# Masked attention on one core: the fourth and fifth token tile transposed in the first two steps of the fifth head, the third pair's values behind them

## The reference, cut to what matters

```python
xt = jnp.transpose(x, (0, 2, 1))
q = xt @ Wq.T
qh = q.reshape(B, T, NH, dk).transpose(0, 2, 1, 3)
scores = scale * jnp.einsum('bhqd,bhkd->bhqk', qh, qh)
logits = (scores * cmask + (1.0 - cmask) * NEG) * rmask
attn = jax.nn.softmax(logits, axis=-1)
ctx = jnp.einsum('bhqk,bhkd->bhqd', attn, qh)
out = ctx @ Wo.T
return x + transpose(out)
```

## Time and profile before

| | |
|---|---|
| median of three runs | 1621.71 us (1619.72 to 1621.74) |
| the profiled execution, and its span | 1617.55 us, 1615.8 us |
| TensorE / its weight loads | 95% / 76% of the span |
| GpSimd / VectorE / ScalarE | 83% / 73% / 53% |
| granted TensorE clock, mean | 0.981 |

### The profile page before, as it was taken

The page is one execution under the profiler, slowest core; times in us unless marked ns, Lnnn a source line. Parts: engine busy times, 40 slices in busy tenths (PEclk is TensorE's granted clock), DMA queues, the critical chain, the costliest instruction groups (busy, mean ns, idle before and its releaser), DMA issues. The chain is left out here.

```text
span 1615.8 us, 33177 instructions
## 1 busy us (share of the span) xinstructions
PE 1537.4 (95%) x10956; PEld 1222.4 (76%) x10956; DVE 1185.3 (73%) x2659; ACT 854.3 (53%) x2055; POOL 1339.1 (83%) x1069
## 2 busy tenths in 40 slices
PE   6798999999999999999999999999999999999995
PEld 3666777787877788787777777777877777777863
DVE  5356787877778787787878778787877778787773
ACT  2145556565555556555555655555555565555450
POOL 5558989898898989889898988989898898987771
PEclk9689999999999999999999999999999999999997
DMA  3434455454544545353554535445554544453410
GB/s 115 107 85 96 105 129 122 110 130 99 129 103 123 122 110 136 93 135 97 123 122 114 136 93 132 100 120 122 123 128 98 129 106 119 115 131 90 109 50 30
DMA packets 93810, 179.09 MB, mean 111 GB/s; under 512 B 24704, under 2 KB 24832, under 8 KB 93632
## 3 DMA queue, kind: packets, MB, share of 16 engines
q1 hardware_dynamic: 64448, 109.71, 30.0%
q0 software_dynamic: 29184, 67.17, 14.9%
HBM read 36.77 MB, written 33.55 MB: 44 GB/s over the span
## 5 line engine op out<-in xcount | busy, mean ns | idle before, releaser
L870 DVE TENSOR_REDUCE small_mxp<-max_scores 108x1 f32<-108x270 f32 x1280 | 546.7, 435 | 269.9 <-PE max_scores L1069 245.4
L751 ACT ACTIVATE small_Pt<-scores,small_kbias 108x270 f32<-108x270 f32 x1280 | 551.5, 483 | 343.9 <-PE scores L1088 335.9
L596 POOL TENSOR_TENSOR small_Pacc<-small_Pacc,small_Pt 108x540 f32<-108x540 f32 x384 | 517.8, 1349 | 117.1 <-ACT small_Pt L751 110.3
L1069 PE MATMUL max_scores<-small_ops 128*108 128x270 f32 x1280 | 412.0, 329 | 17.3 <-DVE small_mxp L870 16.3
L1100 PE MATMUL ctx_psum<-small_Pt,small_V 108*64 108x270 f32 x2560 | 313.1, 391 | 0.0
L900 DVE RECIPROCAL small_rsum<-small_rsum 128x67 f32<-128x67 f32 (+1 forms) x512 | 240.8, 532 | 77.6 <-ACT small_rsum L698 75.8
L1069 PEld LDWEIGHTS max_scores<-small_ops 128*108 128x108 f32 x1280 | 218.9, 173 | 86.3 <-issue 41.0
L1085 PE MATMUL scores<-small_ops 128*108 128x270 f32 x1280 | 270.8, 290 | 4.7 <-ACT small_Pt L751 4.5
L1100 PEld LDWEIGHTS ctx_psum<-small_Pt,small_V 108*64 108x64 f32 x2560 | 184.3, 137 | 106.9 <-issue 0.2
L1088 PE MATMUL scores<-small_ops 128*108 128x270 f32 x1280 | 263.6, 287 | 0.0
L1085 PEld LDWEIGHTS scores<-small_ops 128*108 128x108 f32 x1280 | 191.5, 173 | 25.5 <-ACT small_Pt L751 8.8
(11 more groups left out here) (108 smaller groups left out, 2366.2 us busy)
## 6 DMA issues: line engine op xcount, KB each, us to landing
small_ops<-small_H SPq DMA_DIRECT2D x512, 135.0 KB, 2.8
small_ops<-small_L SPq DMA_DIRECT2D x256, 135.0 KB, 2.7
small_ops<-small_mrow SPq DMA_DIRECT2D x128, 2.1 KB
small_xg<-x_rows,small_idx POOLq DMA_INDIRECT x80, 3.9
small_xtail<-x_rows,small_idx POOLq DMA_INDIRECT x80, 4.9
out_rows<-small_xtail,small_idx POOLq DMA_INDIRECT x80, 3.8
out_rows<-small_xg,small_idx POOLq DMA_INDIRECT x80, 3.8
wq_sb<-wq SPq DMA_DIRECT2D x1, 1024.0 KB, 5.3
```

What stands on the lines that cost most here:

```text
L596: nc.gpsimd.tensor_tensor(acc, other, t["Pt"][:R, p0], ALU.add).then_inc(pacc_step, 1)
L751: nc.scalar.activation(t["Pt"][:R, (NT * s + k) % f.NP, half, :], ST[(2 * (NT * h + k) + half) % 3][:R, 0:H], ACT.Exp, bias=t["kbias"][:R, ...
L870: nc.vector.tensor_reduce(t["mxp"][:R, h % 2, m // 2, m % 2:m % 2 + 1], MX[m % 2][:R, 0:H], AX.X, ALU.max).then_inc(mx_red, 1)
L1069: nc.tensor.matmul(MX[m % 2][:R, 0:H], ops[:, OPA, tile_cols(m // 2)], ops[:, OPB, half_cols(m % 2)], start=True, stop=True).then_inc(mx_r ...
```

## The change

Two entries of one table and one of another are altered. In the fifth head, the fourth tile's transposes go from step 1 to step 0 (part 0), the fifth tile's from step 2 behind the group to step 1 (part 0). The third pair's values go from step 0 (first job in part 0, second in part 1) to step 1 part 1 and step 2 part 1, there behind the group. Every engine takes its share of a job from the same tables, so the copies and residuals move along, and the banks are dealt out anew.

```diff
--- before.py
+++ after.py
@@ -43,8 +43,8 @@
     ((3, 3), (3, 4), "out", 4),
     ((4, 3), (4, 3), "proj", (4, 0)), ((4, 4), (4, 4), "proj", (4, 1)), ((5, 3), (5, 4), "proj", (5, 0)),
     ((6, 0), (6, 1), "proj", (5, 1)), ((7, 0), (7, 1), "proj", (6, 0)), ((7, 3), (7, 4), "w", 0)]
-V_STEPS = {1: ((0, 2, 1), (0, 3, 0)), 2: ((4, 0, 0), (4, 0, 1)), 3: ((5, 0, 0), (5, 1, 0)), 4: ((6, 3, 0), (6, 4, 0))}
-XT_STEPS = [(1, 2, 1), (2, 2, 1), (3, 2, 1), (4, 1, 0), (4, 2, 1)]
+V_STEPS = {1: ((0, 2, 1), (0, 3, 0)), 2: ((4, 1, 1), (4, 2, 1)), 3: ((5, 0, 0), (5, 1, 0)), 4: ((6, 3, 0), (6, 4, 0))}
+XT_STEPS = [(1, 2, 1), (2, 2, 1), (3, 2, 1), (4, 0, 0), (4, 1, 0)]
 XBAR_STEP = (6, 2, 1)
 MT_AT = 1
 CTX_HIGH_AT = {(0, 4): 3, (4, 1): 0, (4, 4): 1, (6, 4): 2}
```

## The result

The changed kernel took 1627.99 us (median of six, 1623.98 to 1628.85) against 1621.34 us before (1619.54 to 1621.74), a ratio of 1.0037 with an interval of [1.0025, 1.0050]: slower, by more than the 0.2% of no change. Run again beside the kernel before, it gave 1625.38 against 1620.76, ratio 1.0027 [1.0018, 1.0037]. The time of 1622.1 that I forecast was too low, and "within 0.2%" was the wrong case; the range reached to 1628.0, and that the measured median lies 0.01 us inside it is luck. Of the ten executions of experiment 4's kernel one took 2151.57 us at a mean clock of 0.652, and the ratio given there is of the other nine.

The account below looks back on a forecast made before the run. TensorE's queue was taken to bound each batch. 14 x 0.04 - 1.06 + 0.72 = +0.2 us on the median 1621.71 gave 1621.9, and half the collision (0.2 us) made it 1622.1; range 1616.0 to 1628.0.

Parts of the forecast that it names:

- within 0.2%: Whole kernel: time differs from the kernel before by no more than 0.2%, 3.2 us; chance 0.59.
- What goes: Pair 4's projection (L1133) no longer waits for VectorE's residual (L892) of the last tile: -0.88 us a batch.
- What comes: Fifth head's first two steps: values job waits for the fourth tile's residual, +0.93 us; middle batch nets +0.04 us.
- The sign for it: New wait of values (L1179) for the residual (L892), 14 times, 0.7 to 0.9 us listed idle.
- What the moved work passes: Fifth head: row sums and group stay hidden by 0.3 and 0.5 us; GpSimd's step 3 sum comes later.
- Off TensorE's path, at nothing: GpSimd's step 3 sum, at about 710.05 instead of 709.22, is absorbed by its later jobs and costs nothing.
- Collision: VectorE's context residual (L905) overlaps GpSimd's later token sum, ending up to 1.0 us later: 0 to +0.3 us a batch.
- The sign for C: L905's mean above 900 ns, for the rival where TensorE pays the collision, 0.1 to 0.6 us a batch; chance 0.22.
- The rule on the ports: VectorE and GpSimd share SBUF ports under an exclusive lock; by it the hold of L905 is certain where they overlap.
- First batch: The 0.73 us wait goes and two matmuls replace four transposes, GpSimd's wait covering the new chain: -1.06 us.
- Last batch: No transposes or projection; the eight values matmuls leave a place where TensorE then waits for VectorE's reduction: +0.72 us.

Follow-up runs that it names:

- experiment 4: Changed kernel with VectorE's second finishing operation (L948) of the fifth output tile cut to 2 of 512 columns; 1620.67 us, ratio 0.9984 to the kernel before.
- experiment 9: Changed kernel with third pair's values back ahead of the transposes, and VectorE's first context residual (L905) moved from (4, 4) to (4, 3); 1610.16 us, ratio 0.9935.
- x10_after_low: Changed kernel with VectorE's first context residual (L905) moved from (4, 4) to (4, 3); 1621.83 us, ratio 0.9999 to the kernel before.
- x5_keep_v_swap: Changed kernel with values back ahead of transposes, GpSimd's token sums of (4, 3), (4, 4) exchanged with scatters of (5, 0), (5, 1); 1721.44 us, ratio 1.0622.
- experiment 12: The changed kernel run again unaltered, for the spread, beside the kernel before; 1625.38 us (1622.77 to 1628.84).
- x6_swap: Changed kernel with GpSimd's token sums of (4, 3), (4, 4) exchanged with its scatters of (5, 0), (5, 1); 1728.21 us, ratio 1.0662.
- x11_before_low: Kernel before with VectorE's first context residual (L905) moved from (4, 4) to (4, 3); 1621.92 us, ratio 1.0008.
- x7_before_swap: Kernel before with GpSimd's token sums of (4, 3), (4, 4) exchanged with its scatters of (5, 0), (5, 1); 1640.30 us, ratio 1.0126.

## Why the prediction was right in part and wrong in part, by its steps

- **What goes:** right. L1133 no longer waits for L892 in any batch, and the wait that was put at 0.88 us was worth that: experiment 9, which has no stall in its place, lasts 92.80 us a batch against 93.66 in most batches before.
- **What comes:** right. Values 3.37 us behind the head's start by the sum (703.45 - 700.08), 3.29 measured; the projection 8.84 to 8.90 by the sum, 8.83 measured. Experiment 4 shows that it hangs on VectorE's finishing operations. Trace and sum agree within 0.1 us because all durations came from rows of the same stretch. With the collision out of the way (x10_after_low) a batch is 0.08 us shorter than before, where the sum had +0.04 with bounds of -0.15 and +0.25. The sign for it, a listed wait of L1179 in every batch, failed, though what it stood for came.
- **What the moved work passes:** the row sums and the group stand for nothing new, as said. GpSimd's sum for step 3 comes 9.99 us behind the head's start instead of 9.14, the 0.85 us that were forecast. "Off TensorE's path, at nothing" is the step that failed: it was at nothing for the row sums, and not for L905.
- **Collision:** the term that was mis-sized, and paid at another place. The prediction bounded it at 0 to 0.3 us a batch and then put half of that, about 0.2 us, into the whole sum, where it belongs into each of 14 batches: its own half would have been 2.1 us and the forecast 1624.0. Measured are 0.37 us a batch for the holds (0.30 net), 4.2 us net in 14. Its mechanism was right for the first place (0.80 us measured, up to 1.0 forecast), but what it left to be paid there, about 0.3 us, was in fact nothing. The second place, which it didn't follow, is held 0.40 us and paid, because GpSimd's next token sum has moved too. That 0.3 a batch stands in both is luck. The sign for C, a mean of L905 above 900 ns, came true: 1084 ns, 808 before.
- **The rule on the ports:** the rule of the Trainium skill that the prediction weighed (SBUF — State Buffer, "SBUF: two separate sides", an exclusive lock on the pair of ports shared by VectorE and GpSimd, held for the whole instruction by the one that starts first) agrees with the holds of the changed kernel, where each ends 0.57 us behind the end of a token sum (719.20 + 1.51 against 720.14, 722.64 + 1.11 against 723.18). It doesn't give the 6.87 us of x5_keep_v_swap, where VectorE stays held over four more instructions of GpSimd that start behind it. Which of two starts first, rows 0.03 us apart don't settle. I should have let the rule set the likeliest case. That it is this lock and no other bond of the two engines, no run here shows.
- **First batch:** -1.06 us forecast; +2.33 in the first profiled execution of the changed kernel and +0.27 in the second. The stall that goes did go. What covers the gain is the clock's lower level, which the profile of before doesn't have there, and the forecast had no such term. In the second execution it came at a place where TensorE would have waited for GpSimd anyway. Why it comes, and whether the changed kernel has it more often, is open.
- **Last batch:** +0.72 us forecast, +0.76 from the wait at (6, 1) of the batch before to the first output matmul of the last (103.14 - 102.38). The wait that takes the place of the values is 0.67 us ahead of the odd maximum of (4, 1), at 1555.58. The row that the forecast reckoned from, at 1554.08, belongs to the sixth head and not to the fifth; that the size came out is luck.

Sum of what the traces show: 4.2 + 0.76 = 4.9 us, and 0.3 to 2.3 us of the first batch. The two comparisons have 6.65 and 4.62 us between their medians. In experiment 12 the executions at a mean clock of 0.979 or more have medians 2.9 us apart (1623.42 and 1620.48), those below it 4.9 (1626.48 and 1621.61). The profiled executions of the changed kernel are also 3.9 and 3.4 us late at the first listed wait for a maximum, before any moved job. That is start-up and not the change: x6_swap, with the same tables for the moved jobs, is only 0.4 us late there, and x11_before_low, without the change, 2.6.

## What to carry to other kernels

When work moves in a kernel whose engines are all near full, redo not only the waits but the overlaps: list the VectorE operations with two inputs in SBUF and what GpSimd does at the same moment, before and after. Moving a job so that it no longer waits for an engine is worth nothing if its bank is handed to it by the same engine; ask which order leaves each bank to the job whose releaser is done first. A hold costs nothing where idle time of the held engine follows (+0.80 us in (4, 4)), and is paid in full where none does (+0.87 us in (5, 1) of x7_before_swap).

## What was not expected of the hardware

- VectorE's operation with two SBUF inputs can be held across several GpSimd operations: 6.87 us behind five without a gap (x5_keep_v_swap), where in the changed kernel it got in after one (1.51 us). In 13 batches of x5_keep_v_swap its row starts from 0.03 us ahead of GpSimd's first to 0.02 behind it, and it is held over all five each time; in x7_before_swap it is held over five where it starts 0.08 us ahead, and gets in after one in the 13 batches where it starts 0.3 us into a sum. One batch of x6_swap breaks the pattern: 0.01 us ahead, and in after one (1.89 us). What decides is open.
- The issue of a scatter on GpSimd doesn't hold it: the first L905 of x5_keep_v_swap, at 750.16, takes 0.71 us beside the scatter at 750.01.
- GpSimd is held by VectorE in its turn: 1.86 us for a sum of 1.35, which is what brings the second collision of the changed kernel.
- A VectorE operation over 2 of 512 columns, with its wait for the one before, still takes 0.38 us.
- TensorE's clock is at its lower level for some microseconds of the first batch in most profiled executions here, of versions of either kernel. What it costs depends on what it covers: about 2 us at 146 to 152 us in the first profile of the changed kernel, some 0.3 us at 128 to 140 us in the second.
